# Tile 3's causal mask added by VectorE in a fused add-and-max, one instruction a head product, with new engine orders

## What is computed

```
q = (x @ wq.T) in 16 heads of width 64;  k, v = one shared head
q = rmsnorm(rope(q));  k = rmsnorm(rope(k))
mask = (cols <= rows) & (rows - cols <= 128)
scores = where(mask, q @ k.T / 8, -1e30)
attn = softmax(scores);  out = (attn @ v) @ wo.T
```

## Time and profile before

| | |
|---|---|
| median of 3 runs | 554.77 us (554.67 to 555.02) |
| the profiled execution's own time | 553.2 us |
| its span | 551.4 us |
| PE matmul busy | 513.4 us (93%) |
| DVE busy | 381.6 us (69%) |
| ACT busy | 313.9 us (57%) |
| POOL busy | 226.6 us (41%) |
| DMA | 6.33 MB, mean 11 GB/s |

### The profile page before, as it was taken

One profiled execution on the slowest core, in us unless ns is written; L12 is line 12 of the kernel. 1 busy time (PEld: TensorE's weight loads), 2 busy tenths in 40 slices (PEclk: granted clock), 3 DMA queues, 4 the chain that ended last, 5 costly groups with the idle time before them and its releaser, 6 DMA issues.

```text
span 551.4 us, 15016 instructions
## 1 busy us (share of the span) xinstructions
PE 513.4 (93%) x6132; PEld 385.6 (70%) x6139; DVE 381.6 (69%) x1209; ACT 313.9 (57%) x645; POOL 226.6 (41%) x234
## 2 busy tenths in 40 slices
PE   8987899899999999999999999999999999999745
PEld 4534567678767876788778877887678767876622
DVE  2658969975997489946995699569965794463120
ACT  2325466565866575658557666667664765453311
POOL 2306743562456145634373526443561356220010
PEclk9999999899999999999999999999999999999976
DMA  7000000000000000000000000000000000000000
GB/s 286 2 7 0 2 7 3 2 2 8 2 3 10 8 2 1 12 7 3 2 12 1 3 2 8 5 2 2 4 8 3 2 3 8 3 2 11 1 0 8
DMA packets 6452, 6.33 MB, mean 11 GB/s; under 512 B 4208, under 2 KB 5744, under 8 KB 6256
## 3 DMA queue, kind: packets, MB, share of 16 engines
q1 hardware_dynamic: 6384, 5.37, 3.1%
HBM read 4.31 MB, written 0.79 MB: 9 GB/s over the span
## 4 chain that ended last, share of the span: by engine, by line
PE 48%; DVE 32%; POOL 8%; ACT 6%; issue 2%; DMA 2%; SPq 1%; POOLq 0%; ACTq 0%; DVEq 0%
PE bank L1023 40%; PE bank L1051 9%; DVE negm L664 5%; DVE q_sb L594 5%; DVE tb L594 5%; DVE ssq L610 4%; POOL qs L833 4%; DMA sh_r<-mT 2%; DVE on L681 2%; POOL rsD L765 1%; POOL rsB L765 1%; DVE tb L481 1%; ACT p L982 1%; DVE ix L714 1%; SPq L395 1%
## 5 line engine op out<-in xcount | busy, mean ns | idle before, releaser
L664 DVE TENSOR_REDUCE negm<-bank 128x2 f32<-128x384 f32 (+1 forms) x128 | 78.8, 615 | 28.3 <-PE bank L1023 27.7
L796 POOL TENSOR_TENSOR q_sb<-q_sb,tb 128x1024 f32<-128x1024 f32 x24 | 57.1, 2380 | 90.5 <-DVE tb L594 90.5
L982 ACT ACTIVATE p<-bank 128x512 f32<-128x512 f32 x112 | 66.0, 601 | 47.0 <-PE bank L1023 45.2
L833 POOL TENSOR_TENSOR qs<-q_sb,qs 128x1024 fp32r<-128x1024 f32 x24 | 57.3, 2387 | 78.2 <-ACT qs L852 78.2
L1023 PE MATMUL bank<-kh,qT 128*128 128x128 f32 (+1 forms) x384 | 79.6, 316 | 0.0
L1023 PE MATMUL bank<-vx,p 128*64 128x65 f32 x1536 | 69.5, 226 | 1.6 <-DVE on L681 0.6
L1023 PEld LDWEIGHTS bank<-vx,p 128*64 128x64 f32 x1536 | 60.0, 138 | 12.0 <-DVE on L681 4.9
L852 ACT ACTIVATE qT<-bank 128x512 fp32r<-128x512 f32 x96 | 53.6, 591 | 24.9 <-PE bank L1051 24.4
L1023 PEld LDWEIGHTS bank<-kh,qT 128*128 128x128 f32 x384 | 62.4, 194 | 1.7
L1023 PE MATMUL bank<-sh_r,sh_l 128*128 128x512 f32 x112 | 50.0, 446 | 3.2 <-DMA sh_r<-mT 3.1
L677 DVE RECIPROCAL rec<-bank 128x4 f32<-128x4 f32 (+1 forms) x88 | 15.7, 179 | 51.6 <-PE bank L1023 51.3
(11 more groups left out here) (165 smaller groups left out, 1066.0 us busy)
## 6 DMA issues: line engine op xcount, KB each, us to landing
wts<-weights SPq DMA_DIRECT2D x1, 1313.0 KB, 6.4
h<-txt SPq DMA_DIRECT2D x1, 672.0 KB, 7.5
img<-images SPq DMA_DIRECT2D x8, 72.0 KB, 1.9
q_sb<-wqkv SPq DMA_DIRECT2D x1, 576.0 KB, 8.5
sh_r<-mT SPq DMA_DIRECT2D x32, 4.0 KB
out<-o_sb SPq DMA_DIRECT2D x8, 64.0 KB, 1.7
p<-masks SPq DMA_DIRECT2D x1, 480.0 KB, 9.4
cst<-shapes SPq DMA_DIRECT2D x1, 352.0 KB, 3.6
```

The lines of the kernel that those rows point to most:

```text
L664: ve.tensor_reduce(dst, src, AX_X, ALU.max, negate=True).then_inc(s_vec, 1)
L796: return gp.tensor_tensor(a, a, b[:, :, ::-1], ALU.add)
L833: gp.tensor_tensor(qs[:, :, D:2 * D], ta[:, t, 0:NH, :], qs[:, :, 0:D].bitcast(F32), ALU.subtract).then_inc(b_pool, 1)
L982: ac.activation(dst.rearrange("s h t -> s (h t)"), bank[BANK_E[n % 2]][:, :], ACT.Exp).then_inc(e_act, 1)
```

## The change

Four edits are made together.

- For the third tile TensorE no longer multiplies the mask in. `b_s` on VectorE runs, for each of the two 192-column products, one `tensor_tensor_reduce` that adds `mask2` (bf16, SBUF) to the scores in PSUM in place and takes the row maximum into `negm` (with its sign kept). The compiler makes two instructions of each: the operation, and one that reads out the accumulator.
- ScalarE's copy of the third tile's `negm` to `mT` multiplies by -1.
- `MERGE` has other orders for all engines.
- `WARM` has 138 idle products in place of 187 (for `xT2` of pair 0: 22 in place of 45).

```diff
-WARM = {("A", "rows", 0): 6, ("A", "cols", 0): 1, ("A", "xT1", 0): 18, ("A", "s01", 0): 3, ("A", "s2", 0): 2, ("A", "ctx", 0):
-        1, ("A", "xT2", 0): 45, ("A", "route", 0): 2, ("A", "h1a", 0): 17, ("A", "h1b", 0): 8, ("A", "y", 0): 2, ("A",
...
+WARM = {("A", "rows", 0): 6, ("A", "cols", 0): 3, ("A", "tok", 0): 2, ("A", "xT1", 0): 18, ("A", "s01", 0): 3, ("A", "s2", 0):
+        1, ("A", "ctx", 0): 1, ("A", "xT2", 0): 22, ("A", "route", 0): 2, ("A", "h1a", 0): 12, ("A", "h1b", 0): 8,
...
-    "gp": "A W3 A2 B A B6 A2 B6 A B4 A2 B6 D B2 A B4 A2 B6 D B2 A B4 A2 B6 D B2 A B4 A2 B6 D B2 A B4 A2 B6 D B2 A B4 "
+    "gp": "A2 W2 A W B A B5 A B A B4 A B5 A B A B7 D B A B3 A B A B7 D B A B3 A B A B7 D B A B3 A B A B7 D B A B3 A "
...
                     else:
-                        src = bank[BANK_S][:, 0:2 * T].rearrange("q (h s) -> q h s", h=2)
-                        dst = negm[:, 32 + 2 * (n - 8):34 + 2 * (n - 8)]
+                        for j in range(2):
+                            s, at = bank[BANK_S][:, T * j:T * j + T], 32 + 2 * (n - 8) + j
+                            ins = ve.tensor_tensor_reduce(s, s, mask2[:, :], 1.0, 2.0 * NEG, ALU.add, ALU.max, negm[:, at:at + 1])
+                        ins.then_inc(s_vec, 1)
+                        return
                     ve.tensor_reduce(dst, src, AX_X, ALU.max, negate=True).then_inc(s_vec, 1)
...
-                    copy(mT[32 * t:32 * t + 16, :], bank[BANK_S][0:16, 0:P]).then_inc(mt_act, 1)
+                    if t < 2:
+                        copy(mT[32 * t:32 * t + 16, :], bank[BANK_S][0:16, 0:P]).then_inc(mt_act, 1)
+                    else:
+                        ac.activation(mT[32 * t:32 * t + 16, :], bank[BANK_S][0:16, 0:P], ACT.Copy, scale=-1.0).then_inc(mt_act, 1)
...
-                        mm(bS[:, 0:2 * T], ident_b[:, :], mask2[:, :].unsqueeze(1).broadcast_to([P, 2, T]), True, False)
                         for j in range(2):
                             h = 4 * i + 2 * j
                             ins = mm(bS[:, T * j:T * j + T], qT2[u][:, b, h:h + 2, :].rearrange("k h t -> k (h t)"), kh[u][:, b, :],
-                                     False, j == 1)
+                                     True, True)
```

## The result

| | before | after |
|---|---|---|
| median of 7 runs each | 554.67 us (552.97 to 555.48) | 556.96 us (556.26 to 557.99) |
| ratio of the medians | | 1.0046, 95% interval 1.0031 to 1.0062 |
| the profiled execution, its span | 553.2, 551.4 us | 557.99, 556.2 us |

What follows compares the result with a forecast made beforehand. No single engine was taken to bound the kernel: rounds of 58.0 us held VectorE's, TensorE's and norm legs. 553.2 - 13 (rounds) - 4.4 (start) - 1.0 (tail) = 534.8; the median lay 1.6 higher: 536.5 us forecast, range 526 to 549.

Steps and rivals of the forecast that it cites:

- it should cease to be the bound: The old loop of 58.0 us a round falls to 56.5 or below; TensorE's own work, 51.2 to 55.8, then binds.
- the 56.0 us a round: Forecast length of a repeating round: a gain of 2.0 us, 1.4 from the mask and 0.6 from waits.
- The signs that were to show it: Expected in the changed kernel's profile: marks 56.0 us apart, rank1 near 21.9, PE above 48% of chain, VectorE busy +20 us.
- The mask product: Third tile's S steps on TensorE: dropping the product saves 0.17 us each, eight a pair, 1.4 us a round.
- The fused operation: Third tile's maxima on VectorE: the fused pair costs 0.56 us against 0.46, +0.10 a step, +0.8 a round.
- no overlap: Rival: VectorE's fused operations do not overlap, +0.31 us a step, a round of 57.7, 547.5 us in all; chance 0.15.
- dear in-place write: Rival: VectorE's write to bank 3 is dear, 0.49 us each, a round of 59.4, about 559.5 us; chance 0.08.
- 2.33 us less: GpSimd's order: lo2 moves ahead of D ln and leaves the norm leg, taking 2.33 us off that leg.
- The start: Pair 0: ctx and ln2 go before the conversions, so rank1 starts near 21.9 instead of 26.27, a gain of 4.4 us.
- The 26 idle products ... at nothing: TensorE's idle products that go outside the start: counted at no cost, because they filled waits.
- The tail: Last pair: its eight mask products are worth 1.4 us, VectorE's S steps take 0.8 more; 1.0 us gain counted.
- All my cases: Forecast of 531 to 541 us (0.63), tight packing at 526.5 (0.14), no overlap (0.15), dear in-place write (0.08).

Runs made afterwards that it cites:

- e2: The kernel before with the new orders and idle products, mask still multiplied in by TensorE and a plain reduction on VectorE: 561.54 us.
- e5: The kernel before with the third tile's mask product left out and its plain reduction kept, so no mask in those maxima: 554.94 us.
- e6: The changed kernel with one plain reduction a step in place of the fused operations, third tile's maxima unmasked: 554.46 us.
- e1: The changed kernel's code with the orders and idle products of the kernel before: 561.74 us.
- e12: The kernel before with all sixteen S steps' maxima taken over only 32 columns a head: 545.94 us.
- e9: The changed kernel without any mask in the sixteen S steps, neither TensorE's products nor VectorE's fused mask, plain reductions throughout: 553.17 us.
- e11: The changed kernel with all sixteen S steps' maxima, fused ones too, taken over only 32 columns of each head or head product: 549.55 us.
- e7: The changed kernel with the mask product of the other eight S steps (S0 to S7) left out too: 553.83 us.
- e8: The kernel before with one edit in GpSimd's order, lo2 ahead of D ln in the repeating rounds: 574.8 us.
- e10: The changed kernel with GpSimd's lo2 put behind D ln again, nothing else: 581.14 us.
- e4: The kernel before with only the start reordered (conversions behind A ctx and A ln2 of pair 0, 22 idle products for 45): 552.15 us.
- e3: The changed kernel with 24 more idle products at places of pairs 0 to 2 where TensorE stood idle: 554.64 us.

## Why the prediction was wrong

**Code and orders, side by side** (medians in us, each beside before at 554.3 to 554.7):

| tile 3's maxima | old orders | new orders |
|---|---|---|
| mask by TensorE, plain reduction | 554.4 (before) | 561.5 (e2) |
| no mask, plain reduction | 554.9 (e5) | 554.5 (e6) |
| mask by VectorE, fused | 561.7 (e1) | 557.0 (after) |

The products are worth nothing in the old orders and 7.1 us in the new ones; the fused operations cost 6.8 in the old and 2.5 in the new. So the orders do move the leg of S8 to S15 from VectorE to TensorE, as forecast, and the change is consistent: in the new orders the trade is a gain of 4.6. But the new orders by themselves cost 7.1.

**The step that failed** is "it should cease to be the bound, and TensorE's own work takes over: between ... 51.2 and ... 55.8 us", and the 56.0 us a round taken from it. Measured were 58.6. TensorE did take over, and its own work was taken too low. By the two readings that gave the bounds (the round less its weight loads' waits, and the matmul rows), and by an estimate explained below, over one round each in us:

| | round | weight loads wait for other engines | round less these waits | matmul rows cover | waits that cost (estimate) | own work by it |
|---|---|---|---|---|---|---|
| before | 58.0 | 5.4 | 52.6 | 57.15 | 1.9 | 56.1 |
| old orders, short maxima (e12) | 57.0 | 2.4 | 54.6 | 56.41 | 1.1 | 56.0 |
| new orders, old code (e2) | 59.3 | 3.2 | 56.1 | 58.38 | 1.6 | 57.7 |
| after | 58.65 | 4.2 | 54.4 | 57.65 | 1.8 | 56.8 |

The first three rows have the same products, and "the round less the waits" is 52.6, 54.6 and 56.1 us: it isn't an amount of work. Idle time of the weight loads isn't idle time of TensorE. Four products of 384 columns and what follows them, first in the kernel before (timelines of PE and PEld, 351.5:353.3), where the next load waited for ScalarE:

```profile
351.92 0.87 PE L1023 MATMUL bank<-xaT,wts 128*64 128x384 f32 x4
352.73 0.74 PE L1023 MATMUL bank<-wts,oT 128*64 128x64 f32 x18
...
352.73 0.66 PEld L1023 LDWEIGHTS bank<-wts,oT 128*64 128x64 f32 x20 [0.61 <-ACT oT L852]
```

and in the changed kernel (360.5:362.3), where it waited for no other engine:

```profile
360.95 0.87 PE L1026 MATMUL bank<-xaT,wts 128*64 128x384 f32 x4
361.75 0.39 PE L1026 MATMUL bank<-mask,ident_b 128*128 128x512 bf16 x1
...
361.74 0.10 PEld L1026 LDWEIGHTS bank<-mask,ident_b 128*128 128x128 bf16 x1 [0.60 <-issue]
```

The next product starts 0.81 us behind the first of the four there and 0.80 here. Of the 0.61 us that the forecast took off TensorE's work, 0.01 was lost time. The last two columns are an estimate in this way: wherever a named wait falls, the distance from one product's start to the next, less the usual distance between such products in these traces where no wait falls. It is good to some tenths of a us, and before and e12, which have the same order on TensorE, agree in it (56.1 and 56.0).

So two things were wrong. There were about 1.9 us of waits to win in a round, not up to 5.4, and the new orders won 0.1 of them. And the new orders make the same products dearer, by about 1.6 us, of which the code gives some 0.9 back. One part of that can be seen: a product of 512 columns of E costs 0.23 us behind another of 512 columns and 0.34 behind narrow ones (start to start, changed kernel):

```profile
346.89 0.39 PE L1026 MATMUL bank<-sh_r,sh_l 128*128 128x512 f32 x1
347.12 0.40 PE L1026 MATMUL bank<-qT,kh 128*128 128x512 f32 x1
...
348.59 0.50 PE L1026 MATMUL bank<-sh_r,sh_l 128*128 128x512 f32 x1
348.93 1.09 PE L1026 MATMUL bank<-qT,kp 128*128 128x512 f32 x4
```

Of a round's fourteen `sh_r,sh_l` six stand behind another of 512 columns before and three after; together they take 3.88 and 4.17 us, 0.3 of the 1.6. Which exchange in the orders makes the rest was not isolated and stays open. TensorE's stream isn't the only bound either: with the other eight mask products gone too (e9) the round is still 58.2, and 5 us less on VectorE leave 57.9 (e11), where the old orders with eight mask products more reach 57.0 (e12).

**The signs that were to show it** nearly all came true: rsB follows rsD with no `qs` between, PE has 73% of the chain, the fused rows read as forecast, the weight loads wait 4.2 us a round (under 5.4), and for `negm` or `bank` of VectorE's maxima 1.3, under the 2.6 that would have spoken against it. They tested the path and not the length of TensorE's stream. Off were the marks (58.6, not 56.0), rank1 (below) and VectorE's busy time, up by 0.9 us and not by 20; 4.9 us less in `wsel` (last section) hides a part of that.

**The mask product, "1.4 us a round".** The column count was right to look at, its worth not. e2 to e6, where only the eight products differ, is 59.3 to 58.4, 0.9 a round or 0.11 a step, where 0.17 was forecast. That the old orders would give nothing was right (e5). mask01's eight products were worth 0.2 in the new orders (e7), so the worth depends on the step's place more than on its columns.

**The fused operation.** The two fused operations of one S step in VectorE's timeline, and what follows them:

```profile
321.52 0.35 DVE L661 CUSTOM_DVE_ANT_0 bank<-bank,mask 128x192 f32<-128x192 f32 x1
321.79 0.14 DVE L661 DVE_READ_ACCUMULATOR2_ANT negm<- 128x1 f32 x1
321.79 0.40 DVE L661 CUSTOM_DVE_ANT_0 bank<-bank,mask 128x192 f32<-128x192 f32 x1
322.11 0.14 DVE L661 DVE_READ_ACCUMULATOR2_ANT negm<- 128x1 f32 x1
322.11 0.25 DVE L703 TENSOR_TENSOR p<-bank,wts 128x96 f32<-128x96 f32 x1
```

The successors start 0.27 and 0.32 us after their starts, the pair takes 0.59: +0.13 a step, forecast +0.10. The step was right, and the two rivals on it (no overlap, dear in-place write) are refuted. By the Trainium skill's page "VectorE: DVE Perf Modes", section "The DRAIN you can't avoid", the next operation waits for the pipe to empty, and, in a clause that the prediction passed over, one that is not held starts earlier. The trace agrees with the clause and not with the rule: the successor starts at 0.27 of 0.35 us. What I didn't price is where those 1.0 us fall: in the old orders all eight steps lie in the leg that binds, and they cost 6.8 us over the program (e1 against e5).

**lo2, "2.33 us less".** It left the norm leg, as forecast: no `qs` stands between rsD and rsB, and neither is on the chain of the round any more. Counting it as a gain that stands by itself was wrong. Alone in the old orders it costs 20 us (e8), since hi2 isn't ready in time; undone in the new orders it costs 24 (e10). Its place before fits the old orders and its new place the new ones, of the two sets tried.

**The start, "-4.4 us, which nothing behind it can take back".** The changed kernel's start:

```profile
15.84 0.29 PE L1026 MATMUL bank<-xpad,h1T 128*64 128x65 f32 x4
...
16.17 0.18 DVE L503 RECIPROCAL recA<-bank 128x3 f32<-128x3 f32 x1 [5.31 <-PE bank L1026]
...
19.73 1.11 ACT L870 ACTIVATE xf<-h,nmA,rsA 128x64 f32<-128x64 f32 x3 [2.69 <-POOL nmA L770]
...
23.14 0.29 DVE L527 CUSTOM_DVE_ANT_0 eq<-bank,fst 128x128 f32<-128x128 f32 x1 [2.23 <-PE bank L1026]
```

rank1 starts at 23.14, not 21.9: the last ctx products now start at 15.84, where before idle products began at 14.54, so `recA` comes at 16.17 and not at 14.6. They are late from `xa` on (ScalarE, 10.49 against 8.98 in the kernel before), ahead of everything that the forecast looked at. The nine traces with the new start differ in this place: rank1 starts between 21.97 (e11) and 23.25 (e7), and in the five with the old start between 26.27 and 28.34. So the 1.2 us by which it missed here are no more than executions vary by. The legs behind `recA` (3.56 and 3.41 us) were as forecast. A gain of 3 us or more is real: in e4 the first D ln is 3.1 sooner and the median 2.3 lower. The step that failed is "nothing behind it can take back": in the changed kernel the first D ln is 4.1 late. Between rank1 and that mark 7.2 us are lost again in the two profiled executions (some two of them may be the executions'); the clock is 2.3 of it by e3's median, and the rest was not separated.

**"The 26 idle products ... at nothing"** was wrong. TensorE waits there in the changed kernel, and the clock falls behind it:

```profile
49.71 1.24 PE L1026 MATMUL bank<-p 128*128 128x512 bf16 x5
54.34 0.72 PE L1054 MATMUL bank<-ident_r,ks 128*128 128x128 f32 x6 [3.39 <-DVE ks L650]
```

After 3.4 us without work (49.71 + 1.24 to 54.34) the products that follow run in a stretch of clock 0.74. e3 prices it at 2.3 us.

**The tail, "-1.0".** Measured +0.6 behind the last D ln, and -1.6 over the two distances ahead of it: -1.0 together, though in other places than forecast. That the sum fits is luck: behind the last mark the traces of the experiments vary from 23.5 to 24.0 with no order in it.

**Summed:** forecast -13 (rounds), -4.4 (start), -1.0 (tail). Measured by the two spans: +1.7 for the five full rounds, +4.1 for the start, -1.0 for the end, 4.8 together, of which the medians show 2.3. On chances: 0.07 for slower was far too little. All my cases shared one premise, that the orders were a gain and only the operation uncertain.

**The version that beats both** is e4, the old rounds with the new start: 552.15 us.

## What to carry to other kernels

Breaking the loop that binds frees only the time in which the next engine really stands still. For TensorE the waits of its weight loads (5.4 us a round here) overstate it, since its matmuls run on meanwhile (about 1.9 us were lost). The same products also took about 1.6 us more in another order, so the sum of an engine's work isn't carried over from one order to another. A change that comes with new orders is best tried as a table of code by orders; here either alone cost 7 us and together 2.3. Idle products that fill a wait are not free to move: ask of each place that loses them how long TensorE would stand still there.

## What was not expected of the hardware

A VectorE operation on 128x3 elements took 2.27 us once. All eight `wsel` (min, median and max in ns), and then the long one with GpSimd's operation beside it:

```profile
L547 DVE SCALAR_TENSOR_TENSOR wsel<-rank,wcol x8: 160/162/2265, 27.0 to 415.5; 128x3 f32<-128x3 f32 x8
```

```profile
119.59 2.27 DVE L547 SCALAR_TENSOR_TENSOR wsel<-rank,wcol 128x3 f32<-128x3 f32 x1
...
119.49 2.35 POOL L833 TENSOR_TENSOR qs<-q_sb,qs 128x1024 fp32r<-128x1024 f32 x1 [1.15 <-ACT qs L852]
```

It ends as GpSimd's operation does (121.86 and 121.84), and TensorE waits 2.24 us behind it, with the clock at 0.83 in 120:130. The traces of all fourteen kernels have 112 such operations. The 62 that start while no GpSimd operation is under way take 0.16 us. The other 50 start while a `qs` runs and end 13 to 22 ns after it, whether that makes them 0.45 or 2.3 us long. Operations of VectorE that read PSUM aren't held so: all 232 `eq<-bank,fst` that started during a long GpSimd operation ended before it. This agrees with what the Trainium skill's page "SBUF — State Buffer", section "SBUF: two separate sides", says of the port pair that VectorE and GpSimd share: against a GpSimd operation that reads SBUF, a VectorE operation with two SBUF inputs finds the pair taken for the whole instruction. In the kernel before, seven of the eight `wsel` fall on lo2 and average 1038 ns over the eight, here 425: the new orders freed VectorE of this in the rounds, and moved the one long wait to pair 1's, where TensorE feels it.
